# One stream over attention and feed-forward of all layers, and an out projection over two batches

## What is computed

```python
def shift_tokens(t):            # second half of the features moved by one token
    a, s = jnp.split(t, 2, -1)
    s = jnp.pad(s, ((0, 0), (1, 0), (0, 0)))[:, :-1]
    return jnp.concatenate([a, s], -1)

def attn_layer(x, Wqkv, qs, ksc, Wo):      # 16 heads of 64
    q, k, v = heads(jnp.split(x @ Wqkv, 3, -1))
    q = l2norm(q) * qs
    k = l2norm(k) * ksc
    q = q * cos * scale + rotate_half(q) * sin * scale
    k = k * cos / scale + rotate_half(k) * sin / scale
    return merge(local_attention(q, k, v)) @ Wo        # window of 32 tokens

def ffn_layer(x, g, bln, W1, b1, W2, b2):
    xn = (x - mu) / jnp.sqrt(var + 1e-05) * g + bln
    a, gate = jnp.split(xn @ W1 + b1, 2, -1)           # 341 columns each
    return a * jax.nn.gelu(gate, approximate=False) @ W2 + b2

for i in range(6):
    x = attn_layer(shift_tokens(x), Wqkv[i], q_scale[i], k_scale[i], Wo[i]) + x
    x = ffn_layer(shift_tokens(x), ln_g[i], ln_b[i], W1[i], b1[i], W2[i], b2[i]) + x
```

## Time and profile before

| | us |
|---|---|
| median of 3 runs (lowest, highest) | 4304.59 (4303.39, 4310.63) |
| the profiled execution | 4307.25 |
| its span, from the first instruction to the last | 4305.4 |
| TensorE busy | 4041.0 (94%) |
| VectorE busy | 3601.2 (84%) |
| ScalarE busy | 3057.7 (71%) |
| GpSimd busy | 3010.0 (70%) |

### The profile page before, as it was taken

The page is one execution under the profiler, slowest core; times in us unless marked ns, Lnnn a source line. Parts: engine busy times, 40 slices in busy tenths (PEclk is TensorE's granted clock), DMA queues, the critical chain, the costliest instruction groups (busy, mean ns, idle before and its releaser), DMA issues.

```text
span 4305.4 us, 111689 instructions
## 1 busy us (share of the span) xinstructions
PE 4041.0 (94%) x30864; PEld 3177.6 (74%) x30864; DVE 3601.2 (84%) x12077; ACT 3057.7 (71%) x11197; POOL 3010.0 (70%) x3393
## 2 busy tenths in 40 slices
PE   7888887899998999989999999999899999999998
PEld 5777776688876888767888768887578886688875
DVE  5676665899978999968999789999699997899985
ACT  1455544788864888838888658888388885588883
POOL 2333332799965999928999659999299995699980
PEclk9999998999999999999999999999999999999998
DMA  4222221000000000000000000000000000000000
GB/s 146 80 79 79 79 85 56 6 0 0 0 21 7 1 0 0 0 21 7 0 0 0 21 7 1 0 0 0 26 1 0 0 0 21 7 0 0 0 0 20
DMA packets 75916, 82.96 MB, mean 19 GB/s; under 512 B 13622, under 2 KB 69396, under 8 KB 74836
## 3 DMA queue, kind: packets, MB, share of 16 engines
q1 hardware_dynamic: 75732, 80.87, 5.8%
HBM read 45.33 MB, written 35.52 MB: 19 GB/s over the span
## 4 chain that ended last, share of the span: by engine, by line
PE 79%; DVE 9%; issue 5%; ACT 4%; POOL 2%; DMA 0%; DVEq 0%; SPq 0%; POOLq 0%; ACTq 0%; PEldq 0%
PE bank_pair L981 11%; PE bank L992 10%; PE bank L1007 9%; PE bank L1015 8%; PE bank L456 8%; PE bank L972 7%; PE bank L458 6%; PE bank L457 6%; PE bank_pair L1203 2%; PE bank_pair L560 1%; PE bank L554 1%; PE bank L536 1%; DVE uf L1351 1%; ACT p L637 1%; ACT sc L626 1%
## 5 line engine op out<-in xcount | busy, mean ns | idle before, releaser
L1064 ACT ACTIVATE p<-p,mx 128x128 f32<-128x128 f32 x3072 | 1195.9, 403 | 46.9 <-DVE mx L1115 45.7
L1152 POOL TENSOR_TENSOR rot<-own_crossed 128x512 f32<-128x512 f32 x768 | 984.7, 1282 | 29.6 <-DVE own_crossed L1090 29.6
L1162 POOL TENSOR_TENSOR p<-p,ri 128x512 f32<-128x512 f32 x768 | 801.7, 1044 | 54.8 <-DVE ri L1112 54.0
L1146 POOL TENSOR_TENSOR rot<-rot,rn 128x512 f32<-128x512 f32 x768 | 803.7, 1046 | 0.0
L1115 DVE CUSTOM_DVE_ANT_0 p<-bank_pair,band_f 128x128 f32<-128x128 f32 x3072 | 692.1, 282 | 5.6
L1064 ACT ACTIVATION_READ_ACCUMULATOR p<-p,mx 128x1 f32 x3072 | 617.3, 201 | 0.0
L1122 DVE COPY pTl<-bank 128x512 f32<-128x512 f32 x768 | 530.3, 691 | 89.2 <-PE bank L1007 83.7
L456 PE MATMUL bank<-wqkv_hi,xs_lo 128*128 128x512 f32 x1152 | 563.4, 489 | 40.5 <-POOL xs_lo L1135 21.7
L1044 ACT ACTIVATE qkT<-bank 128x512 f32<-128x512 f32 x768 | 454.2, 591 | 173.9 <-PE bank L972 173.8
L981 PE MATMUL bank_pair<-qkT 64*128 64x128 f32 x6144 | 549.4, 297 | 3.8 <-DVE mx L1115 3.1
L992 PE MATMUL bank<-pTl,v_sb 128*64 128x128 f32 x6144 | 512.0, 288 | 24.6 <-DVE zS L1097 19.9
(11 more groups left out here) (195 smaller groups left out, 7253.1 us busy)
## 6 DMA issues: line engine op xcount, KB each, us to landing
pos_scratch<-pos_sb SPq DMA_DIRECT2D x32, 1020.0 KB, 4.3
sc<-pos_scratch SPq DMA_DIRECT2D x32, 512.0 KB, 4.0
own_crossed<-in_L_ffn_Wqkv SPq DMA_DIRECT2D x6, 1536.0 KB, 6.7
ctx_sb<-in_ctx SPq DMA_DIRECT2D x32, 128.0 KB, 3.5
wo<-in_L_ffn_Wo SPq DMA_DIRECT2D x6, 512.0 KB, 7.1
mrow<-in_mask_BxS_fk SPq DMA_DIRECT2D x1, 2048.0 KB, 7.7
x_all<-in_x SPq DMA_DIRECT2D x4, 512.0 KB, 8.7
out<-res SPq DMA_DIRECT2D x8, 256.0 KB, 2.3
```

Of the source, the lines that this page charges most:

```text
L1064: last = nc.scalar.activation(p[:, j, h, :], p[:, j, h, :], ACT.Exp, bias=mx[:, j, h:h + 1], scale=-1.0, accum_out=psums[:, j, h:h + 1])
L1146: nc.gpsimd.tensor_tensor(rot[:, j4, :, :], rot[:, j4, :, :], rn[:, jr, (k - 4) % 2, :].unsqueeze(2).to_broadcast([128, 2 * G, DL]), ALU.m ...
L1152: nc.gpsimd.tensor_tensor(rot[:, j4, :, :], own[:, j4, :, :], crossed[:, j4, :, :], ALU.add).then_inc(L["rot0"], 1)
L1162: nc.gpsimd.tensor_tensor(p[:, j, :, :], p[:, j, :, :], ri[:, j, :].unsqueeze(2).to_broadcast([128, G, T]), ALU.mult).then_inc(L["pn"], 1)
```

## The change

One stream takes the place of the two pipelines and of the loop over layers around them. A body is one quad, that is 16 units. Attention of quad q of a layer stands beside the feed-forward of the quad two before it, across layers too: the first two quads of a layer run beside the feed-forward of the last two of the layer before. Attention is 16 steps deep. The bodies are laid out as: two, then a loop over layers with a loop of 6 quads and two bodies of the next layer, then 6 quads of the last layer, and two bodies that empty the stream (the last has only feed-forward).

The feed-forward is written anew for this. The centred value comes in one product with identity minus 1/128 (centre_w), the variance in one product of 512 columns (which leaves it in every row), the root by Ln and Exp on ScalarE, gain and shift on ScalarE, two products on GpSimd. All its products and the v projection share bank 2 and hand it to each other in turn; the gate is copied out by VectorE before the gelu, which works in place. Each quad has one table load for gelu and one back. The out projection takes two batches: 8 products of 256 columns into the second half of bank 3, once in 8 units, with oT twice as long. Wqkv has memory of its own, is split in six groups at the turn of a layer (ScalarE high, GpSimd low part), and the weight loads of the next layer wait for the last use of each tile. The core of the diff:

```diff
-            pipeline(pe, UNITS, 8, SKEW, emit, peeled=2, beside=beside)
...
+        def stream(eng, emit):
...
+            def body(l, q):
+                for k in range(BODY):
+                    emit(l, q, k)
+            body(0, 0)
+            body(0, 1)
+            with eng.Fori(0, LAYERS - 1) as l:
+                with eng.Fori(2, QUADS) as q:
+                    body(l, q)
+                body(l + 1, 0)
+                body(l + 1, 1)
+            with eng.Fori(2, QUADS) as q:
+                body(LAYERS - 1, q)
+            body(LAYERS - 1, QUADS)
+            body(LAYERS - 1, QUADS + 1)
...
+                if on(9) and k % 2 == 1:
+                    if at.ffn(15):
+                        pe.wait_ge(L["z"], QUADS + at.F + 1)
+                    elif at.ffn(1, 3, 7, 9, 11, 13):
+                        gone, each, done = SHARED_AHEAD_OF_V[k]
+                        pe.wait_ge(Fm[gone], each * at.F + done)
...
+                    two = oT[:, (k - 22) % 16:(k - 22) % 16 + 2 * UB, :].rearrange("p (b u) n -> p b u n", b=2)
                     for c in range(OUT_CHUNKS):
+                        last = nc.tensor.matmul(y_ps.rearrange("p (b n) -> p b n", b=2), wo[:, c, :], two[:, :, c // 2, c % 2 * T:(c % 2 + 1) * T],
+                                                start=(c == 0), stop=(c == OUT_CHUNKS - 1))
...
+                if at.ffn(10):
+                    gelu(1)
+                    gelu(2)
+                    use_table(LOG_EXP_SET)
...
+                if at.ffn(9):
+                    use_table(GELU_SET)
+                    gelu(0)
```

More of the change, by code:

```diff
@@ new lines, in emit @@
+                if on(9):
+                    pe.wait_ge(L["rot"], n(9) + 1)
+                    if at.again(9, 1):
+                        pe.wait_ge(L["qkT"], n(9))
+                    for c in range(4):
+                        last = nc.tensor.transpose(qkT_ps[:, c * T:(c + 1) * T], rot[:, (k - 9) % 4, 2 * c:2 * c + 2, :].rearrange("p h n -> p (h n)"), ident[:, :])
+                    last.then_inc(L["T1"], 1)
+                if at.ffn(6):
+                    v_gone()
+                    pe.wait_ge(Fm["w1_split"], at.lf + 1)
+                    pe.wait_ge(Fm["xn"], at.F + 1)
+                    gate(0)
@@ L1055, in emit @@
[L1055 to L1062 removed]
+                    if at.again(7, 8):
+                        act.wait_ge(L["rot"], n(7) - 6)
@@ new lines, in emit @@
+                if at.ffn(12):
+                    value(2)
+                if on(5):
+                    if at.again(5, 4) and k % 2 == 1:
+                        dve.wait_ge(L["clamp"], at.pair(5) - 1)
+                    nc.vector.tensor_reduce(ss[:, (k - 5) // 2 % 2, (k - 5) % 2, :], sq[:, (k - 5) % 2, :, :], X_AXIS, ALU.add).then_inc(L["ssum"], 1)
+                if at.ffn(8):
+                    keep_gate(2)
+                if at.ffn(14):
+                    dve.wait_ge(Fm["y_mm"], at.F + 1)
+                    for rows, kept in kept_halves(at.ffn_batch(), QUAD):
+                        last = nc.vector.scalar_tensor_tensor(kept, ffn_ps[rows, :].rearrange("p (a n) -> p a n", a=QUAD), b2c[rows, :], kept, ALU.add, ALU.add)
+                    last.then_inc(L["z"], 1)
```

881 lines of the change are left out of this document (405 added, 476 removed).

## The result

The changed kernel takes **4407.1 us** (median; 4404.5 to 4408.5), the kernel before 4305.2 us beside it (4303.4 to 4310.6): 1.0234 times as long, 95% interval 1.0216 to 1.0252, or 102 us more. The prediction had the sign, and 52 of the 102 us. The profiled execution took 4408.5 us with a span of 4406.5.

The account below looks back on a forecast made before the run. TensorE was taken as the bound. 763.9 ahead, 48 quads x 71.9 (3451), 45 fill and drain, 30 turns, 48 waits and 20.5 tail gave 4358 us, less 0.8: about 4357, 1.2% slower; range 4220 to 4450.

Parts of the forecast that it names:

- The work per unit: TensorE's attention units: more switches between full and part array cost 0.175 us per unit on average, 134 us in all.
- Rival 1: TensorE's attention units: the array's switch is hidden and the stream wins, 4223 us; chance 0.30 with half-way cases.
- The waits in a quad: TensorE waits 1 us per quad for ScalarE or bank 2, 48 us in all; bounds 0 and 3 us (144).
- Rival 2: Within quads: ScalarE's burst or bank 2 limits, 3 us per quad instead of 1, 4453 us; chance 0.14.
- The turn of a layer: At 5 turns: 3.7 us for jumps, 2.3 for Wqkv groups, 6 us a turn, 30 in all; bounds 0 and 60.
- fill and drain: Kernel before, each layer: TensorE short of work for 31.0 us; 186 us over six layers is the most to win.
- The ends: The one stream's single filling and emptying: 31.0 us scaled by 16/11 to 45 us.
- The 256 columns at nothing: Out projection, 8 products of 256 columns per two batches: 0 us; bounds a gain of 55, a loss of 18.
- rival 3: Inner loop of 16 units: instructions refetched at each of 36 turns, 35 to 130 us, 4437 us; chance 0.09.

Follow-up runs that it names:

- experiment 2: The changed kernel with the scores put back between the transposes of q and k and the product with v: 4393.9 us, 1.0207.
- experiment 3: The changed kernel with GpSimd's roundings of Wqkv moved from the head of its step to the end: 4386.3 us, 1.0189.
- both edits: The changed kernel with GpSimd's roundings last in their step and the scores back between transposes and product with v: 4374.5 us, 1.0159.

## Why the prediction was right in sign and short in size

**The work per unit, the term that I thought decides: right.** 71.9 us of TensorE per quad were predicted and 71.9 found, and not by chance: the unit shown has the predicted length too. Torn apart in the kernel before, the pair costs 101 us, near the 0.15 x 768 = 115 of its two edges. Rival 1 (a hidden switch) is out. But the prediction let this term bear the whole verdict, and experiment 2 corrects that: with the pair together again the quad is 72.3, not 69.9. Putting the pair together wins 0.4 us a quad in one order and 1.0 in the best one tried, and even without table loads the quad stays at 71.15. So a free switch would hardly have given rival 1's 4223; that is argued, as no run has one.

**The waits in a quad: sized a little too high.** 1 us taken, 0.75 measured, 12 us over 48 quads. VectorE and GpSimd came out within 1.2 us of their sums and ScalarE within 0.3. Rival 2 with its 3 us did not come, but waits for ScalarE show as soon as TensorE is relieved.

**The turn of a layer: the step that failed.** "6 us a turn, 30 us in all; bounds 0 (all hidden in the queues) and 60." It measured 83.3 us for the five turns and 13.5 for the four jumps, 97 in all, outside the bounds. The jumps stayed under the 18.5 that they were priced at; the turns did not stay near 11.5. The prediction named the place ("GpSimd stands first in line for what ScalarE does last in such a step") and priced it at 2.3 us. It priced the roundings as work. They are five waits, 16.0 us of GpSimd's time, with the division of p queued behind each: experiment 3 took 4.1 to 5.7 us of a turn away by moving lines alone. VectorE's tables, unpriced at 1.0 us for both, took 2.7 in the changed kernel's first turn and 10.6 with both edits, where VectorE was held until GpSimd ran dry. And 3.9 us of the first turn are TensorE at the lower clock after its gaps. Before, the roundings stood beside the feed-forward, and the tables at the layer's start, where GpSimd was idle. How much of the 31.0 us per layer that I booked as "fill and drain" was such preparation, which does not go away with the drain, no run shows.

**The ends: too high.** The stream starts at 757.9 us, 6 earlier than the stages did; that is luck, since the start lies between 757 and 764 us in the kernels here, for no reason that I know. Of the span, 757.9 ahead, 48 x 72.65 = 3487, 97 for turns and jumps and 7 for the last layer's slower loop leave 58 us, 20.5 of them taken for the tail as before: some 37 for fill and drain against 45.

**Together:** 4358, less 12 (waits), 8 (ends) and 6 (start), plus 67 (turns and jumps) and 7 (the last layer's loop), is 4406 for a span of 4406.5. It must come out so, because the ends are what the other terms leave.

**The 256 columns at nothing:** right within 11 to 19 us in the stream, a gain. The bound below was kept open for that. Alone in the kernel before, with the addition and the order that go with them, they cost 29 us, which no row of the product's own duration could tell.

**Fetch (rival 3):** five of six layers' loops run without it, at 72.65 us. The jump of the layer loop shows four times, as 1.8 to 2.4 us ahead of the scores. VectorE's loop of 266 instructions thus stays whole there; only the last layer's copy, the same lines, shows fetches in every quad, and its quads take 7 us more in all. The prediction read the rule of the Trainium skill ("Runtime: NRT & Kernel Launch", Instruction fetch mechanics) too strictly: two blocks of 256 instructions are 512, so that a loop of 266 is over the edge only where it reaches into a third block. Whether that is so for the last copy, no run here shows.

No variant beat the kernel before. The best, at 4329 us, has the pair together, the scores at the head of the step, GpSimd's roundings last and the tables on GpSimd; it lacks 0.6%.

## To carry over

Price an engine's work in a moved step by what is queued behind its first wait, not by its duration: weight preparation that sat in a stage of its own becomes a ring of waits in a full stream. When one engine bounds and the next is within a few per cent, removing the bound wins only the gap between the two, so measure the second bound before counting the gain (here 16 x 0.13 = 2.1 us of TensorE per quad were worth 0.4). And, as far as one run can teach it, keep the bounding engine's extra work in small pieces, often, if another engine is slower than it in between: 3.46 us once in eight units lost 29 us against 1.79 once in four.

## What was unexpected in the hardware

- A product of VectorE on two SBUF operands took 0.69 us beside an idle GpSimd. Beside one that worked without a break it took 0.68, 1.53 or 7.66 us: either GpSimd's own operation became longer (0.71 for 0.27 us), or VectorE was held past one operation after another until GpSimd ran dry. In the changed kernel its products that read PSUM kept their 0.69 behind it (1327.50), beside a busy GpSimd.
- Between products on the whole array and products on 64 of its rows or columns TensorE loses 0.06 to 0.09 us at each change, 0.13 us per unit for one pair torn apart. It shows as "issue" ahead of weight loads: 136.8 us ahead of the scores' before, 287.6 with the pair torn apart.
- Around two waits of 3.95 and 4.31 us, 15 us apart, the granted clock was 0.70 and 0.83 over 10 us, and scores that take 0.72 us took 1.23 after each.
